# Eight GpSimd scatters of slots moved behind the q and k powers, in a post-norm model of a state-space layer, two MLPs, a gated cumulative layer and a mixture of experts

## The reference, cut to what matters

```python
x = _layernorm(x + _L0_attn_ref(x, ...))   # state-space layer: 64 heads of 8, state 64, chunked scan
x = _layernorm(x + _L0_ffn_ref(x, ...))    # gated MLP, 704 wide, weights of small integers
x = _layernorm(x + _L1_attn_ref(x, ...))   # q, k, v; RMS of q and k; cumulative sums; gated MLP, 1024 wide
x = _layernorm(x + _L1_ffn_ref(x, ...))    # mixture of 16 experts, 4 chosen for each token
```

```python
q = _rms(q); k = _rms(k); w = jnp.exp(k)
y = jax.nn.sigmoid(q) * (cumsum(w * v) / (cumsum(w) + 1e-06))
```

## Time and profile before

| What | Value |
|---|---|
| median of 3 runs | 2281.87 us (2273.9 to 2294.1) |
| the profiled execution | 2266.03 us, its span from the first to the last instruction 2263.6 us |
| mean granted TensorE clock | 0.931 |
| busy | PE 1892.4 us (84%), DVE 1363.3 (60%), POOL 823.4 (36%), ACT 760.0 (34%) |
| indirect DMAs of `layers_block` | 112 gathers, 115.9 us of POOL; 128 scatters, 129.4 us of POOL |

### The profile page before, as it was taken

One profiled execution on the slowest core, in us unless ns is written; L12 is line 12 of the kernel. 1 busy time (PEld: TensorE's weight loads), 2 busy tenths in 40 slices (PEclk: granted clock), 3 DMA queues, 4 the chain that ended last, 5 costly groups with the idle time before them and its releaser, 6 DMA issues. The chain is left out here.

```text
span 2263.6 us, 35897 instructions
## 1 busy us (share of the span) xinstructions
PE 1892.4 (84%) x9588; PEld 1340.7 (59%) x9589; DVE 1363.3 (60%) x3020; ACT 760.0 (34%) x1527; POOL 823.4 (36%) x823
## 2 busy tenths in 40 slices
PE   3698988979879889879889797746899999999990
PEld 2366756656657557557566575433566666666660
DVE  3777867867768767768677685322344444444445
ACT  3334423434334344334343342211233322223223
POOL 2124134134143142141341431222455555555554
PEclk7799999999999999989999998877999999999995
DMA  8123223123123033131231230019633333333337
GB/s 280 52 74 98 62 69 98 57 65 106 38 84 97 25 100 98 29 98 57 69 102 38 84 93 21 19 33 286 166 62 56 61 60 59 58 58 61 58 54 230
DMA packets 155390, 187.60 MB, mean 83 GB/s; under 512 B 38672, under 2 KB 134224, under 8 KB 154960
## 3 DMA queue, kind: packets, MB, share of 16 engines
q1 hardware_dynamic: 110288, 115.44, 16.2%
q0 software_dynamic: 40704, 67.40, 14.9%
q10 hardware_dynamic: 4352, 4.20, 0.5%
HBM read 119.23 MB, written 67.73 MB: 83 GB/s over the span
## 5 line engine op out<-in xcount | busy, mean ns | idle before, releaser
L1619 PE MATMUL pu<-w_ug,xh 128*128 x1728 | 360.5, 357 | 20.8 <-issue 11.9
L1758 POOL DMA_INDIRECT sums_dram<-yo,meta_in x144 | 228.0, 1583 | 253.0 <-DVE yo L1728 238.3
L1712 DVE TENSOR_TENSOR gate_hid<-pu,gate_hid 128x448 f32<-128x448 f32 x144 | 90.0, 625 | 360.3 <-ACT gate_hid L1680 356.6
L1619 PEld LDWEIGHTS pu<-w_ug,xh 128*128 128x128 bf16 x1728 | 168.7, 99 | 169.0 <-issue 45.4
L793 PE MATMUL pb<-x1T,w_sw 128*128 128x256 f32 x1024 | 231.1, 385 | 0.7 <-ACT x1T L911 0.7
L1680 ACT ACTIVATE gate_hid<-pu 128x448 f32<-128x448 f32 x144 | 78.3, 544 | 454.8 <-PE pu L1619 422.4
L793 PEld LDWEIGHTS pb<-x1T,w_sw 128*128 128x128 f32 x1024 | 196.0, 193 | 44.4 <-ACT x1T L911 10.8
L1645 PE MATMUL py<-w_dn,hh 112*128 x1728 | 215.2, 274 | 1.1 <-DVE yo L1728 1.1
L1645 PEld LDWEIGHTS py<-w_dn,hh 112*128 112x128 bf16 x1728 | 168.6, 98 | 22.3 <-issue 1.9
L999 POOL TENSOR_SCALAR yss<-yss 128x2 f32<-128x2 f32 x16 | 3.7, 232 | 459.2 <-ACT sq_a L898 459.2
L1748 POOL DMA_INDIRECT xin<-x_dram,meta_in x144 | 141.9, 986 | 74.5 <-issue 42.0
(11 more groups left out here) (246 smaller groups left out, 3565.4 us busy)
## 6 DMA issues: line engine op xcount, KB each, us to landing
w_stage<-in_w_ug SPq DMA_DIRECT2D x64, 224.0 KB
split_ug<-w_parts SPq DMA_DIRECT2D x64, 224.0 KB
w_ug<-split_ug SPq DMA_DIRECT2D x16, 896.0 KB, 13.9
xg_dram<-xg SPq DMA_DIRECT2D x16, 512.0 KB, 3.6
rows<-sums_dram SPq DMA_DIRECT2D x32, 256.0 KB, 5.5
w_stage<-in_w_dn SPq DMA_DIRECT2D x32, 224.0 KB
split_dn<-w_parts SPq DMA_DIRECT2D x32, 224.0 KB
w_dn<-split_dn SPq DMA_DIRECT2D x16, 448.0 KB, 14.8
```

Of the source, the lines that this page charges most:

```text
L1619: last = mm(pu[:, 2 * b + w, 0:EH], xh[:, b, xp, c, :], w_ug[:, bass.ds(e, 1), wp, c, w * EH:(w + 1) * EH], start=n == 0, stop=n == 3 * DC ...
L1712: vec.tensor_tensor(hid[:, m % 2, :], pu[:, 2 * (m % 2), 0:EH], gate, ALU.mult).then_inc(hid_ready.sem, 1)
L1758: nc.gpsimd.indirect_dma_start(out=sums_dram[m % 2], out_offset=bass.IndirectOffsetOnAxis(ap=meta[:, m, 0:1], axis=0), in_=yo[:, m % 2, :] ...
```

## The change

The eight scatters of a sequence's slots move in GpSimd's list from in front of the second layer norm's power to behind the power of q and k. No instruction is added, removed or altered, and no other engine's list changes.

```diff
-    "POOL": ("A6- A2 A2L AX.0 AX.1 D8+ B2 G1+ B3 A5 B6"),
+    "POOL": ("A6- A2 A2L AX.0 AX.1 B2 G1+ B3 D8+ A5 B6"),
```

## The result

The changed kernel takes 2163.05 us (median of 4 runs, 2157.7 to 2169.5) against 2277.89 (4 runs, 2270.6 to 2294.1): ratio 0.9488, interval 0.9428 to 0.9548. The profiled execution took 2164.68 us.

A forecast was written before the change was run, and what follows sets the result against it. Late take-up of finished TensorE products was taken to bound the first stage's rounds: 107 us, 18 remaining, so 2266.03 - 89 + 14 = 2191 us profiled, 2207 us as median (3.3% faster); range 2166 to 2320.

The forecast's parts named there:

- What bounds the kernel, and whose hold it is: First-stage MLP: finished TensorE products are taken up late (the hold) in rounds having both gathers and scatters, lengthening each round.
- Rival A: Old place: the run of fifteen indirect DMAs makes the hold; cutting it dissolves most; 2207 us, chance 0.47.
- The three kinds of round: First stage: round 1 (gathers only) and 16 (scatters only) show no hold; rounds 2 to 15, with both, do.
- The size of the hold: Excess waits of Silus (86.8 us) and down-projection sums (20.5): together 107 us, 7.7 in each of 14 rounds.
- The new place, 14 us: Behind the q and k power: scatters meet a weight transfer and TensorE's work, costing 1 us a round, 14 us.
- The 15.8 us on top: Whole kernel: the median of runs lay 15.8 us above the profiled execution; this was added to the forecast.
- What is left in the old place (18): Old place: part of the hold begins before any scatter; 2 us in each of nine rounds stay, 18 us.
- Nothing for the queue: GpSimd's old place: emptying the queue by 10.24 us gains nothing, since the norm's power waits for VectorE by 9.57 us.
- The new place's cover: Ahead of the state-space layer's power: 28.7 us of GpSimd idleness a round; scatters fit free, leaving 18 us.
- B: Hold follows the scatters, from meeting SyncE's weight transfers; 8.6 us a round in the new place; 2313 us, chance 0.23.
- C: New place: a hold that ends with the weight transfer itself, some 4 us a round; 2249 us, chance 0.15.
- D: Old place: gathers and weight transfers make the hold, scatters only lie there; 2282 us, give or take 12; chance 0.15.

The follow-up runs named there:

- the dummies: Changed kernel plus eight small gathers, results unread, in the scatters' old place, in a batch with a hold: 2289.05 us, ratio 1.0099 to the kernel before.
- the sixteen in the new place: Changed kernel plus eight small gathers, results unread, straight behind the scatters in the new place: 2304.03 us, ratio 1.0157 to the kernel before.
- the eleven: Kernel before with four of the eight scatters moved to the new place, four left behind the seven gathers, with a hold: 2212.20 us, ratio 0.9751.
- before_again: The kernel before, unchanged, profiled again in a later batch without a hold: 2167.14 us, ratio 0.9993.
- after_again: The changed kernel, unchanged, run again in a later batch without a hold: 2150.40 us, ratio 0.9920 to the kernel before.
- pieces_away_5: Kernel before with SyncE's weight pieces and their casts moved away from gathers and scatters, in a batch with a hold: 2298.07 us, ratio 1.0103.
- pieces_away_3: Kernel before with SyncE's weight pieces and their casts moved away from gathers and scatters, without a hold: 2182.60 us beside 2167.89.
- behind_b2: Kernel before with all eight scatters moved behind the second layer norm's power, ahead of the next two powers: 2224.64 us, ratio 1.0259; again 2226.88, 1.0288.

## Why the prediction was wrong

**What bounds the kernel, and whose hold it is.** Right in kind for the measurement that it was made for: TensorE's finished products were taken up late, and cutting the run of fifteen ended most of that. Rival A's mechanism holds. The three kinds of round pointed to it, and the dummies, the sixteen in the new place and the eleven show it.

**Where the time went, by stretches.** The starts of four instructions cut each round into stretches. Here they are in us, summed over the 16 rounds, from the profiles of the two kernels with a hold and without:

| Stretch | before, hold | before_again, none | after, hold | after_again, none |
|---|---|---|---|---|
| first product of the MLP (line 731) to its sum (line 1334) | 425.0 | 319.2 | 330.3 | 319.4 |
| that sum to the norm's power (line 1033) | 33.2 | 50.9 | 33.1 | 33.2 |
| norm's power to the q and k power (line 1043) | 193.8 | 184.7 | 187.0 | 185.6 |
| first product of the second MLP (line 793) to its sum (line 1378) | 365.5 | 363.7 | 366.2 | 363.6 |
| all else | 1246.1 | 1241.1 | 1245.8 | 1245.0 |
| span | 2263.6 | 2159.6 | 2162.4 | 2146.8 |

**The size of the hold.** Right: 107 us were forecast from the excess of waits, and the first stretch is 425.0 - 319.4 = 105.6 us longer with a hold, the slower matmuls of the down projection included. In before_again, too, it is 105.8 us shorter. So next to nothing has to be added for the clock that falls in the hold (0.53 in the earlier trace rows), though line 745 was busy for 116.5 us in before and 96.6 in before_again. In rounds 3, 4, 9 and 11 the way from the sixth take-up to the end of the down projection did take 0.4 to 1.1 us more than the 5.9 of before_again. What the prediction left out is small: 8.2 us between the norm's power and that of q and k (193.8 against 185.6). In rounds 2, 6, 8 and 13, the four in which line 849's product is held as well, and in round 3 it is 13.6 to 13.8 us, and in most others 10.8. How that hold reaches the power was not traced.

**The steps that failed.** Two terms of the sum were mis-sized.

- *The new place, 14 us.* The second MLP, where the scatters now stand, grew by 0.7 us from before to after (365.5 to 366.2), and is 2.6 us longer with the hold than without (363.6). What lies between the q and k power and that stretch didn't grow (162.9 us before, 162.5 after). The 1 us a round was chosen near the lower of two bounds; no row gave it. The runs show a take-up at the first Silu that is 0.8 us late (2.87 in place of 2.08) and a next wait that is shorter by about as much (0.55 us; it is 1.34 in after_again).
- *The 15.8 us on top.* The prediction subtracted the hold of the profiled execution and carried over the 15.8 us by which the median lay above it. The profiled execution of before (2266.03 us) was faster than all four timed runs; that of after (2164.68) lies 1.6 us above the median of its own. So 17.4 us of this distance did not carry over, 4.0 of them by the fourth run of the kernel before (2281.87 then, 2277.89 now). Whether the hold was longer in the other executions can't be seen, since each kernel has one profile in a batch.

**What is left in the old place (18).** Right in mechanism, too large: in the first stretch 330.3 - 319.4 = 10.9 us are left. In round 10 the fifth product is taken up 2.7 us later than without a hold (a wait of 3.95 in place of 1.25), but the sixth then follows at once, 0.3 us late, and the sum comes 1.1 us late. A take-up that is late by less than the next ordinary wait costs little. In all, the changed kernel with a hold less the same without is 2163.05 - 2150.40 = 12.7 us (15.6 by the spans), instead of 32.

**The account.** For the profiled execution 2191 us were forecast and 2164.7 measured, 26.3 less: 13.3 us of the new place (14 less 0.7), 5.7 of the old (94.7 gained, from 425.0 to 330.3, instead of 89), 6.8 between the norm's power and that of q and k (193.8 to 187.0), where nothing was forecast, and 0.5 of all else. With the 17.4 us of the median that is the whole 44. All of these errors had one sign, and the two largest are a term taken without a row and one carried over without a reason. The low end of the range, "all 107 us gone, 10 for noise", had the same 15.8 us in it.

**Nothing for the queue.** Right in the batch of the prediction, where the power was 9.57 us early. The rest of that thought, that it would be in the way by 0 to 2 us without a hold, is borne out: 18.1 us in 14 rounds is 1.3 a round, and the table has 17.7 of them in its second row (50.9 against 33.2).

**The new place's cover.** Right: 18.29 us are left behind eight scatters, and 18.16 behind sixteen, whose round had grown with the hold. The rule of the Trainium skill that was weighed (SBUF — State Buffer, "SBUF: two separate sides") did little. The prediction read it as pushing all eight. In round 10 one scatter took 1.40 us and the first 1.10, and the other six took 0.96; the trace doesn't bear that reading out.

**The rivals.** B (the meeting with SyncE's store) falls: eight scatters met that store in the new place and made a wait of 2.87 us, not one of 7.3 to 9.9; and with the pieces gone from the old place, pieces_away_5 has the hold at full size (416.9 us in the first stretch, 316.8 in pieces_away_3). C falls with it. D falls: gathers and pieces stayed, "remote" went.

**What stays open.** Why a batch has a hold or not. It is not the chip, by the numbers that the record gives the chips: 11 had it in one batch and not in another, and so had 12. Within a batch all executions of the kernel before were of one kind. Whether a pause between gathers and scatters is enough to break the run is not shown either, since behind_b2 met no batch with a hold. Nor is it shown what in a run holds TensorE. By the records it is the signal that comes late: the product is at its end, the taker is free, and the wait ends 1.4 to 2.4 us behind the run. The Trainium skill (Perfetto Trace Analysis, "Tensor Engine Instruction (MATMUL, LD_WEIGHTS)") says that a matmul's end in a profile is estimated from its size, while the semaphore rises only when PSUM has acknowledged the bytes, a time that the profile doesn't show. By it the hold would lie in that unseen part; the page names no cause and no such length, and no run here could look into it.

## What to carry to other kernels

A finished TensorE product that is taken up late beside a row of indirect DMAs is a reason to break that row up: here seven and eight apart gained 115 us on fifteen with a hold, and 18 without, the latter by GpSimd's queue alone. Eleven and four did as well only where nothing was held. When you price a stall of TensorE, measure the stretch from the first product to what needs its result: the matmuls behind the stall were 20 us slower here at the lower clock, but mostly beneath the next held product, and the stretch grew by the waits alone. Ask also whether the distance of the median from the profiled execution belongs to what your change removes. And before you explain a difference, run the kernel before once more in another batch: here its time had two values 5% apart, and the change was worth 5% beside one and 0.8% beside the other.

## What the runs showed of the hardware that was not expected

**Two kinds of batch.** The same program took 2166 to 2170 us in five batches and 2265 to 2278 in four (that of the prediction among them). Another mark goes with it, far from the rounds: the experts' loads of `w_ug` landed a median of 7.6 to 9.0 us after their issue in the 13 profiles of the first kind, and 13.2 to 15.9 in the six of the second. The DMA issues of the page (count, KB each, median us to landing), of the kernel before:

```profile
w_ug<-split_ug SPq DMA_DIRECT2D x16, 896.0 KB, 13.9
```

and of before_again:

```profile
w_ug<-split_ug SPq DMA_DIRECT2D x16, 896.0 KB, 7.8
```

**SyncE is slowed beside the run too.** The first and the last of two pairs of store and load, in round 10 of the kernel before, during its gathers:

```profile
898.22 0.60 SPq L576 DMA_DIRECT2D split_ug<-w_parts  x1
...
904.23 0.70 SPq L569 DMA_DIRECT2D w_stage<-in_w_ug  x1
```

and the same two in before_again:

```profile
845.56 0.60 SPq L576 DMA_DIRECT2D split_ug<-w_parts  x1
...
847.93 0.47 SPq L569 DMA_DIRECT2D w_stage<-in_w_ug  x1
```

From one to the other it is 6.0 us in the one and 2.4 in the other. So beside GpSimd's indirect DMAs more than TensorE's signals is late in such a batch; whether the two have one cause was not tried.
